# One attention and feed-forward block on one core: weight splits and bias addition of the first two steps in another order and partly on POOL, the last step's attention rows on DVE

## The reference

```
xn  = (x - mean) / sqrt(var + 1e-5)                       # per row
qkv = xn @ Wqkv.T ; 16 heads of 16 ; q *= 16**-0.5
# segments of 512 rows; keys and values: every 8th row of the segment (64)
scores = q @ k.T ; c = max over each block of 64 query rows, per key
w   = exp(scores - c) ; out = (w @ v) / (sum_k w + 1e-10) ; out @ Wout.T
ffn = relu(xn @ W1 + b1) @ W2 + b2                        # W1 256x1024, W2 1024x256
```

## Time and profile before

| | |
|---|---|
| median of 3 runs | 1140.32 us |
| the profiled execution | 1139.81 us, of which the profile's span is 1138.0 us |
| PE busy | 1109.6 us, 97% |
| DVE, ACT, POOL busy | 66%, 57%, 54% |
| granted PE clock, mean | 0.992 |

### The profile page before, as it was taken

One profiled execution on the slowest core, in us unless ns is written; L12 is line 12 of the kernel. 1 busy time (PEld: TensorE's weight loads), 2 busy tenths in 40 slices (PEclk: granted clock), 3 DMA queues, 4 the chain that ended last, 5 costly groups with the idle time before them and its releaser, 6 DMA issues.

```text
span 1138.0 us, 23173 instructions
## 1 busy us (share of the span) xinstructions
PE 1109.6 (97%) x7457; PEld 939.7 (83%) x7457; DVE 745.6 (66%) x1370; ACT 651.5 (57%) x1078; POOL 619.0 (54%) x488
## 2 busy tenths in 40 slices
PE   5799999999999999999999999999999999999997
PEld 4478988888888888888888888888888888888886
DVE  7777667667666757666667666667666667677540
ACT  4546556556556556555655555655565565555652
POOL 2435555555555555565565556565466465565464
PEclk9999999999999999999999999999999999999999
DMA  6445454444444444445344544444445343544421
GB/s 188 102 116 128 118 130 113 104 114 117 124 125 111 108 107 124 119 115 126 96 119 111 132 109 122 108 111 118 126 102 137 91 126 106 138 100 110 102 76 60
DMA packets 96139, 130.57 MB, mean 115 GB/s; under 512 B 25840, under 2 KB 54128, under 8 KB 96112
## 3 DMA queue, kind: packets, MB, share of 16 engines
q1 hardware_dynamic: 96112, 130.23, 44.8%
HBM read 39.98 MB, written 18.87 MB: 52 GB/s over the span
## 4 chain that ended last, share of the span: by engine, by line
PE 95%; DVE 2%; issue 1%; POOL 1%; POOLq 0%; ACT 0%; DVEq 0%
PE y_bank L738 40%; PE h_bank L738 39%; PE misc L872 6%; PE s_bank L800 5%; PE misc L813 2%; PE misc L738 2%; DVE xn L620 0%; DVE w_exp L635 0%; DVE s_max L629 0%; PE misc L838 0%; PE misc L821 0%; DVE xn_keys L590 0%; DVE w_lo L554 0%; PE s_bank L738 0%; POOL att L394 0%
## 5 line engine op out<-in xcount | busy, mean ns | idle before, releaser
L387 POOL TENSOR_TENSOR h_lo<-h_full,h_hi 128x512 fp32r<-128x512 f32 x256 | 335.7, 1313 | 464.2 <-ACT h_full L453 460.1
L459 ACT ACTIVATE w_exp<-w_exp 128x512 f32<-128x512 f32 x256 | 162.7, 636 | 237.6 <-DVE w_exp L635 237.4
L738 PE MATMUL y_bank<-w_hi,h_hi 128*128 128x256 f32 x1024 | 290.0, 283 | 0.0
L738 PE MATMUL y_bank<-w_lo,h_hi 128*128 128x256 f32 x1024 | 289.8, 283 | 0.0
L738 PE MATMUL y_bank<-w_hi,h_lo 128*128 128x256 f32 x1024 | 289.5, 283 | 0.0
L451 ACT ACTIVATE h_hi<-h_bank,b_cols 128x512 fp32r<-128x512 f32 x256 | 175.8, 687 | 106.5 <-PE h_bank L738 100.9
L629 DVE TENSOR_REDUCE s_max<-s_bank 128x8 f32<-128x512 f32 x256 | 175.4, 685 | 69.8 <-PE s_bank L800 68.0
L738 PE MATMUL h_bank<-xt_hi,w_hi 128*128 128x512 f32 x512 | 211.2, 413 | 2.4 <-DVE q_lo L658 2.4
L738 PEld LDWEIGHTS y_bank<-w_lo,h_hi 128*128 128x128 f32 x1024 | 195.3, 191 | 9.8
L738 PEld LDWEIGHTS y_bank<-w_hi,h_hi 128*128 128x128 f32 x1024 | 194.8, 190 | 9.2
L738 PE MATMUL h_bank<-xt_hi,w_lo 128*128 128x512 f32 x512 | 202.2, 395 | 0.0
(11 more groups left out here) (87 smaller groups left out, 1606.9 us busy)
## 6 DMA issues: line engine op xcount, KB each, us to landing
q_pack<-q_hi SPq DMA_DIRECT2D x256, 128.0 KB, 2.4
x_raw<-x SPq DMA_DIRECT2D x32, 512.0 KB, 3.4
q_pack<-q_lo SPq DMA_DIRECT2D x128, 128.0 KB, 2.4
rden_rows<-rden_dram SPq DMA_DIRECT2D x128, 128.0 KB, 3.5
out<-y SPq DMA_DIRECT2D x32, 512.0 KB, 2.9
k_pack<-k_hi SPq DMA_DIRECT2D x256, 32.0 KB, 1.9
num_den<-num_den SPq DMA_DIRECT2D x32, 256.0 KB, 2.5
k_pack<-k_lo SPq DMA_DIRECT2D x128, 32.0 KB, 1.9
```

Source lines behind the costliest of these rows:

```text
L387: pool.tensor_tensor(h_part[1][:, i % HBUF], h_full[:, i % HBUF], f32(h_part[0][:, i % HBUF]), ALU.subtract).then_inc(h_lo, 1)
L459: act.activation(w_exp[:, pair], w_exp[:, pair], ACT.Exp).then_inc(w_ready, 1)
L738: mm = pe.matmul(ps, stationary[a], moving[b], start=start and c == 0 and n == 0, stop=stop and c == len(pairs) - 1 and n == 2, skip_group ...
```

## The change

1. **SP, start.** The loads of b1, b2 and of segment 1 are issued ahead of the four loads of wout.
2. **POOL, start.** After `inverse_deviation(0)` POOL makes `residual(-1)` (it waits for the second split of DVE and for the constants), then the low part of w1 (formerly on DVE), then `inverse_deviation(1)`, and only then the first hidden tiles. In step -1 `inverse_deviation(2)` stands ahead of the two hidden tiles of the tail, and `residual(0)` stands behind them instead of at the start of step 0.
3. **DVE, start.** w1 is no longer split here. `mean_variance(1)` comes before the split of w2, and wout is split at the end of step -1.
4. **PE.** `EARLY` is 6: a sixth first product of segment 0, and the second product of tile 3, move from step 0 to step -1. The first product waits for w1's own semaphore.
5. **Step 31.** The products and low parts of the attention rows are on DVE, ahead of its last additions. ACT makes their high parts before hidden tile 7. The store is issued in two halves.

```diff
-    EARLY = 5
+    EARLY = 6
@@ SP, first_step
                 sp.dma_start(w2_raw, w2.rearrange("(c p) n -> p c n", p=P)).then_inc(w2_loaded, 16)
+                sp.dma_start(b1_cols[:], b1).then_inc(const_loaded, 16)
+                sp.dma_start(b2_rows[:], b2.partition_broadcast(P)).then_inc(const_loaded, 16)
+                load_x(1, 1)
                 (the four loads of wout)
-                (b1, b2, load_x(1, 1))
@@ SP, step
+                if ffn and not attention:
+                    for b in range(YB):
+                        sp.wait_ge(y_ready, s * YB + b + 1)
+                        sp.dma_start(out_rows[s][:, 2 * b:2 * b + 2], y[:, par, 2 * b:2 * b + 2]).then_inc(y_stored[par], 16)
@@ POOL, step
-                    if i == 2 and attention:
+                    if isinstance(s, int) and s <= 0:
+                        if i == 5 and s == 0:
+                            residual(s, par)
+                    elif i == 2 and attention:
                         residual(s, par)
-                if ffn:
+                if attention and ffn:
                     (attention_out, attention_lo)
+                if isinstance(s, int) and s == -1:
+                    inverse_deviation(s + 3, 1 - par)
@@ POOL, first_step
                 inverse_deviation(0, 0)
+                pool.wait_ge(w_lo, 2)
+                residual(-1, 1)
+                pool.wait_ge(w_hi, 3)
+                pool.tensor_tensor(w1s[1][:], w1_raw, f32(w1s[0][:]), ALU.subtract).then_inc(w1_lo, 1)
+                inverse_deviation(1, 1)
                 for i in range(LAG):
                     hidden_lo(0, i)
-                inverse_deviation(1, 1)
@@ ACT, step: in step 31 ahead of hidden tile 7
+                if ffn and not attention:
+                    for quad in range(QUADS):
+                        attention_hi(s, quad, par)
@@ DVE
+            def last_attention(s, par):
+                dve.wait_ge(rden_rows_in, (s + 1) * 64)
+                dve.wait_ge(num_merged, (s + 1) * 16)
+                for quad in range(QUADS):
...
+                    dve.tensor_tensor(att[:, quad], num_den[:, quad, 0], rden_rows[:, quad],
+                                      ALU.mult).then_inc(att_ready, 1)
+                for quad in range(QUADS):
...
+                    dve.tensor_tensor(att_part[1][:, par, quad], att[:, quad], f32(att_part[0][:, par, quad]),
+                                      ALU.subtract).then_inc(att_lo, 1)
@@ DVE, step
                     mean_variance(s + 3, 1 - par)
+                if isinstance(s, int) and s == -1:
+                    split_lo(len(splits) - 1)
+                if ffn and not attention:
+                    last_attention(s, par)
@@ DVE, first_step
                 drain_kv(-2)
-                split_lo(2)
                 mask_k(-2)
...
-                for w in range(3, len(splits)):
-                    split_lo(w)
                 mean_variance(1, 1)
+                split_lo(3)
@@ PE
-                    pe.wait_ge(w_lo, 3)
+                    pe.wait_ge(w1_lo, 1)
```

More of the change, by code:

```diff
@@ L152, in ln_attention_ffn @@
         w_lo = sem("w_lo")
+        w1_lo = sem("w1_lo")
         x_loaded = [sem(f"x_loaded{i}") for i in range(2)]
@@ L280, in first_step @@
                         sp.dma_start(wout_raw[a::2, c], wout_heads[c, a]).then_inc(w2_loaded, 16)
-                sp.dma_start(b1_cols[:], b1).then_inc(const_loaded, 16)
-                sp.dma_start(b2_rows[:], b2.partition_broadcast(P)).then_inc(const_loaded, 16)
-                load_x(1, 1)
                 for j in range(PAIRS // 2):
@@ L353, in step @@
                     pack(s, 3)
-                if ffn:
+                if ffn and attention:
                     sp.wait_ge(y_ready, (s + 1) * YB)
                     sp.dma_start(out_rows[s], y[:, par]).then_inc(y_stored[par], 16)
+                if ffn and not attention:
+                    for b in range(YB):
+                        sp.wait_ge(y_ready, s * YB + b + 1)
+                        sp.dma_start(out_rows[s][:, 2 * b:2 * b + 2], y[:, par, 2 * b:2 * b + 2]).then_inc(y_stored[par], 16)
             iterations(sp, first_step, step)
-            for par in range(2):
-                sp.wait_ge(y_stored[par], 16 * (NSEG // 2))
+            sp.wait_ge(y_stored[0], 16 * (NSEG // 2))
+            sp.wait_ge(y_stored[1], 16 * (NSEG // 2 + 1))
         @block.gpsimd
@@ L425, in step @@
                     hidden_lo(segment, i)
-                if load:
+                if load and not (isinstance(s, int) and s == -1):
                     inverse_deviation(s + 3, 1 - par)
@@ L643, in invert_den @@
                 dve.reciprocal(rden[:], den[:]).then_inc(rden_ready, 1)
+            def last_attention(s, par):
+                dve.wait_ge(rden_rows_in, (s + 1) * 64)
+                dve.wait_ge(num_merged, (s + 1) * 16)
+                for quad in range(QUADS):
+                    dve.wait_ge(att_hi, (s - 1) * QUADS + quad + 1)
+                    dve.wait_ge(att_lo, (s - 1) * QUADS + quad + 1)
+                    dve.tensor_tensor(att[:, quad], num_den[:, quad, 0], rden_rows[:, quad],
+                                      ALU.mult).then_inc(att_ready, 1)
+                for quad in range(QUADS):
+                    dve.wait_ge(att_ready, s * QUADS + quad + 1)
+                    dve.wait_ge(att_hi, s * QUADS + quad + 1)
+                    dve.tensor_tensor(att_part[1][:, par, quad], att[:, quad], f32(att_part[0][:, par, quad]),
+                                      ALU.subtract).then_inc(att_lo, 1)
             def transposed_lo(s, par):
@@ L768, in second_product @@
                 if isinstance(s, int) and s == 0 and i == 0:
-                    pe.wait_ge(w_lo, len(splits))
+                    pe.wait_ge(w_lo, 3)
                 if 0 in tokens:
@@ L784, in output_product @@
                 pe.wait_ge(att_lo, (s + 1) * QUADS)
+                if isinstance(s, int) and s == 0:
+                    pe.wait_ge(w_lo, 4)
                 for t in range(T):
```

1 line of the change is left out of this document (removed).

## The result

| | before | after |
|---|---|---|
| median of the runs, us | 1140.34 | 1132.84 |
| lowest to highest | 1138.23 to 1140.99 | 1132.34 to 1134.44 |
| profiled execution, us | 1139.81 | 1133.35 |
| its span, us | 1138.0 | 1131.6 |
| start of step 1 in the chain of waits | 83.51 | 82.60 |

Ratio 0.9938, 95% interval 0.9926 to 0.9951. The kernel became 7.5 us faster; 9.0 were forecast, and 1131.3 was expected where 1132.84 came: just above the range with a chance of 0.58 (to 1132.8), inside the wider one (to 1134.8). The last two rows of the table divide the profile's 6.4 us: 5.5 at the end, as forecast, and 0.9 at the start, where 3.5 were.

A forecast was written before the change was run, and what follows sets the result against it. PE's matmuls bound steps 1 to 30, so only start and end could gain: 1139.81 - 5.5 - 3.5 = 1130.8 profiled, 1140.32 - 9.0 = 1131.3 for the median. Range 1129.8 to 1132.8 (chance 0.58), wider 1128.2 to 1134.8.

The forecast's parts named there:

- The end: Step 31: attention rows leave POOL, PE's wait and clock drop go, store in halves; 5.5 us (4.4 to 6.6).
- The 1.7 for the product: Step 31: PE keeps its clock, so the output product takes 2.87 us and not 4.61; saves 1.7.
- The 0.4 for the store: Step 31: storing in two halves saves 0.4 us at the end of the span.
- The rival that the end doesn't come off: Step 31: ACT's copies precede the last hidden tile, rden_rows lands late; end gives 3.5, time 1133.3; chance 0.03.
- w1's split on POOL: Start: the split takes 4.7 us and holds k_lo to 20.5; PE's first hidden product comes at 21.3.
- k_lo is not held: Rival at the start: k_lo runs free, start gives 5.5 to 6.5 us, time 1128.3 to 1129.3; chance 0.12.
- The constants weren't late: Start: b2 lands at 13.2; rival, at 16.5, start gives 0 to 2, time 1133 to 1135.3; chance 0.14.
- Step -1: PE gets 2.82 us more, 2.6 fills idle time; last q_lo 0.5 later (0.4 earlier to 1.3 later).
- The head of step 0: Inverse deviation at 52.0, xn_keys ends at 53.3 and not 56.13, normalisations near 57.9: 2.2 us.
- DVE's 3.8 decides: Step 0: with the 1.62 wait for the keys' product gone DVE gains 3.8 us; PE alone could gain 5.7.
- the rival on the clock: Step 0: PE's gaps put queries and later products at the lower clock; two further microseconds go, 1133; chance 0.09.
- the start term, 3.5: Start, up to step 1: 3.5 us saved, with 0.3 taken off for PE's clock.

The follow-up runs named there:

- end_only: The kernel before with only the edits of step 31; 1134.56 us, ratio 0.9952 to before.
- w1_dve: The kernel after with w1's split back on DVE, ahead of the masking of the keys; 1132.69 us, ratio 0.9931 to before.
- the second profile: The kernel after, unchanged, profiled once more; median 1132.82 us, step 1 at 82.22.
- early5: The kernel after with EARLY back at 5, five hidden tiles ahead of step -1's queries; 1133.19 us, ratio 0.9938 to before.
- start_only: The kernel after with the end as in before, only the edits of the first two steps; 1137.68 us, ratio 0.9983 to before.
- stats_packs: The kernel after with segment 2's loads and statistics early and three of step -1's 24 pack copies on ACT; 1130.97 us, ratio 0.9918 to before.
- warm: The kernel after with six extra thrown-away matmuls on PE ahead of the transposes of step 0; 1132.83 us, ratio 0.9934 to before.
- stats_early: The kernel after with segment 2's loads issued in the first step and its statistics in step -1; 1134.06 us, ratio 0.9941 to before.
- ACT's six: The kernel after with the last six of step -1's 24 pack copies issued by ACT; 1132.21 us, ratio 0.9923 to before.
- ACT's three: The kernel after with three k copies of step -1's last pair group issued by ACT; 1131.99 us, ratio 0.9924 to before.

## Why the prediction came out as it did

The total came near, and the end as forecast. The start did not: by the prediction's own sign (wrong if step 1 starts after 82) it failed, with 82.60 and 82.22.

- **The end: right.** 5.5 forecast, 5.5 in the profile (1054.5 less 1049.0), 5.8 in the runs of end_only. PE's wait went (3.4), the output product takes 3.05 and not 4.61 (1.6), and from DVE's last addition to the end are 2.56 and not 3.08 (0.5). The 1.7 for the product compared two measures: 4.61 runs to the end of the last matmul, 2.87 counts only the distances between them. The 0.4 for the store was a little too small, and the two errors nearly cancel. The rival that the end doesn't come off is out: ACT's copies ran between two tiles and the rows landed by 1115.4.
- **w1's split on POOL: right in size** (4.60 for 4.7), and so is the hold on k_lo (to 20.97 for 20.5). The first hidden product came at 21.72 for 21.3. But this delay is not seen at the end of step -1: with k_lo free and the product 0.7 earlier the last q_lo came no earlier (w1_dve). "k_lo is not held" was priced at 5.5 to 6.5 us for the start; w1_dve, in which DVE still pays for the split, gives no hint of such a gain. The constants weren't late: the addition started at 13.75 for 13.2.
- **Step -1: the step that failed first.** "DVE's last q_lo ... 0.5 later (between 0.4 earlier and 1.3 later)": it came 1.6 later, and 2.2 in the second profile. The queries did run at full clock, as forecast. But PE began them at 43.16, where 41.8 to 42.3 were forecast: its 2.6 us of idle time between 35 and 41 were counted as room for the 2.82 of the product, but with five tiles and the new order (early5) it is idle there for 1.1 only. early5 puts 0.9 of the q_lo's delay on the sixth product (the rest, 0.8, is little more than the 0.5 by which the q_lo of before's order differs between before and end_only), and shows that leaving it out gains nothing, since PE has to do it in step 0.
- **The head of step 0: right.** From the last q_lo to the end of xn_keys 9.6 became 5.9; my numbers gave 6.3.
- **"DVE's 3.8 decides": the step that failed second.** The sum followed one chain through step 0, DVE's, and up to the transposes ahead of the seventh scores it gave what was forecast: from 21.7 to 17.1 behind the last q_lo, 4.6 for 4.3. But SP's row starts from the same q_lo: 21 of the 24 copies, and among them four transfers of the denominators. Its last copy landed 19.6 behind the q_lo in before (it took 4.1 us, where 2.4 is usual) and 17.9 in end_only, which has the same order there, and the seventh scores came 22.48 and 22.04 behind it: 2.9 and 4.1 to spare, less than the 4.3 that the forecast used up. In after one long issue brought the landing to 18.4, and PE lost 0.6 between the transposes and the scores. This was never in the working, which looked at the row only in the first step. Beside it, the rival on the clock was right as a mechanism: it was given 0.09 and a price of 2; the allowance in the forecast was 0.3, and the measured price is 1.4 behind the seventh scores (15.94 less 14.51; 0.6 at least, against all profiles with full clock there) or, in the second profile, a wait of 1.25 for the keys' product. So the start term, 3.5, measured 0.9 and 1.3 in the two profiles, and 1.7 to 2.0 in the runs (after less end_only; start_only less before). In the first profile 1.1 of the shortfall of 2.6 is the late q_lo, 0.6 the copy and 1.15 the clock beyond its 0.3, less 0.3 that DVE gained more than forecast; in the second 1.7 of 2.2 is the q_lo. This says where it arose, not what an edit would win back (early5 won nothing), and copy and clock can't be parted cleanly: the one seems to set off the other.
- The forecast of step 1 "near 80.0" was met by stats_packs, 80.12, where the q_lo is as late as in after but DVE's chain and SP's are both shorter.

The step from before to after is 7.5 in the runs and 6.5 in the profiled executions because before's profiled execution was 0.5 faster than its median and after's 0.5 slower. Open is why single issues of SP took 1.1 to 1.6 us and not 0.60 in five profiles (both of after, start_only, warm, stats_early), and what makes the start vary so from profile to profile: the same k_lo of before's order ended at 19.63 in before and at 20.5 in end_only.

## What to carry to other kernels

When a chain gets shorter, list every other chain that starts at the same event and measure the slack of each: a row of small DMA issues on one queue is such a chain, here 25 of 0.64 us. A shorter chain alone gains nothing if PE only arrives earlier at a wait that stays where it is, and it may cost, if PE comes out of that wait at the lower clock. PE's idle time in the old profile is room for more work only if the change leaves it idle there.

## What the runs showed of the hardware

- The held instruction can be on either engine: POOL's addition over 128x4, 0.21 us in before, took 2.16 when it started 0.16 behind DVE's split of w2. The Trainium skill, "SBUF — State Buffer", section "SBUF: two separate sides", has whichever starts first take the shared pair of ports for its whole instruction; the trace agrees, both here and for k_lo (2.21):
```profile
24.32 2.26 DVE L571 TENSOR_TENSOR w_lo<-w_exp,w_hi 128x2048 fp32r<-128x2048 f32 x1
...
24.48 2.16 POOL L382 TENSOR_TENSOR var_eps<-mean_var,eps 128x4 f32<-128x4 f32 x1 [3.80 <-DVE mean_var L595]
```
- The lower clock showed behind the idle stretch more than in it: in the second profile of after PE was busy 1.52 of 4 us at 0.84, and then 4.00 of 4 at 0.50. The same program met the dip at 58 us in one execution and at 66 in another.
- Beside SP's copies, ACT's six brought the DMA engines to 0.90 busy, and the last copy of a group took 4.1 us to land and not 2.4 (the fifth scores at 63.08 and not 61.51), though before has one copy of 4.1 without a second queue. What a second queue does save is the first queue's issuing, 0.64 us each: ACT's three were worth 0.8 us. The Trainium skill, "DMA: Bandwidth & Descriptors", section "Issuing engines are not separate DMA queues", has the DMAs of all engines run on the same 16 DMA engines and interleave, so that a second issuing engine saves only the time of initiating, "usually small relative to the DMA itself". For one copy that holds here (0.60 us, and it lands in 2.4), for the row it doesn't: its 25 issues stand behind one another and take 16 us.
